# A decoder layer on one core: the attention steps written out, the gate work of a batch shifted to other slots

## The reference

```python
x = _layernorm(x + _L0_attn_ref(x, Wq, Wk, Wv))
x = _layernorm(x + _L0_xattn_ref(x, ctx, ctx, mask, W1, b1, W2, b2))
# in the experts: which two of eight, and with which weight
gate_scores = softmax(einsum('btd,ed->bte', x, Wg))
topk_val, topk_idx = top_k(gate_scores, 2)
topk_val = topk_val / (topk_val.sum(-1) + 1e-9)
comb = (one_hot(topk_idx, 8) * topk_val[..., None]).sum(-2)
x = _layernorm(x + sum_e comb[e] * ((a_e * sigmoid(b_e)) @ Wo.T + bo))
```

## Time and profile before

| | us |
|---|---|
| median of three runs | 1499.45 |
| the profiled execution | 1495.7 |
| its span, first to last instruction | 1493.9 |
| PE busy in the span | 1282.1 (86%) |
| DVE busy | 1142.6 (76%) |
| ACT busy | 756.8 (51%) |
| POOL busy | 656.1 (44%) |

### The profile page before, as it was taken

How to read it: one execution, slowest core, us unless ns; L and a number is a source line. 1 busy time by engine, 2 the same in 40 slices (tenths; PEclk the granted TensorE clock), 3 DMA queues, 4 the chain that set the end, 5 groups by cost and what they waited for, 6 DMA issues and landing times. The chain is left out here.

```text
span 1493.9 us, 32343 instructions
## 1 busy us (share of the span) xinstructions
PE 1282.1 (86%) x7668; PEld 903.5 (60%) x7669; DVE 1142.6 (76%) x3110; ACT 756.8 (51%) x1743; POOL 656.1 (44%) x1018
## 2 busy tenths in 40 slices
PE   6888999989899898989988505999999999968886
PEld 4443555555555555555543304888888888858786
DVE  1455788888788787878874467888888888859998
ACT  1125677777677677777777241323223232314444
POOL 1011244444454444444544472334343343447886
PEclk9998999999999999999998557999999999989999
DMA  4435456647556566566535721433434334369995
GB/s 100 105 60 100 80 107 131 122 103 131 114 113 126 113 119 116 119 124 112 118 87 181 273 94 58 133 135 130 137 128 136 131 129 138 129 239 318 338 331 200
DMA packets 171805, 211.34 MB, mean 141 GB/s; under 512 B 20048, under 2 KB 143056, under 8 KB 167632
## 3 DMA queue, kind: packets, MB, share of 16 engines
q1 hardware_dynamic: 147808, 143.92, 41.7%
q0 software_dynamic: 17680, 55.28, 9.9%
q10 hardware_dynamic: 6240, 11.34, 2.2%
HBM read 124.81 MB, written 84.89 MB: 140 GB/s over the span
## 5 line engine op out<-in xcount | busy, mean ns | idle before, releaser
L859 DVE TENSOR_REDUCE negmax<-psS 128x2 f32<-128x512 f32 x512 | 349.6, 687 | 109.0 <-PE psS L631 102.0
L761 ACT ACTIVATE probs<-psT 128x512 f32<-128x512 f32 x512 | 302.7, 597 | 190.3 <-PE psT L641 189.4
L631 PE MATMUL psS<-kstack,qstack 96*128 96x256 bf16 x1024 | 197.4, 275 | 50.7 <-DVE negmax L859 21.6
L1337 ACT ACTIVATE sig<-hb 128x512 f32<-128x512 f32 x136 | 86.0, 633 | 287.2 <-DVE hb L1420 281.6
L641 PE MATMUL psT<-qstack,kstack 99*128 99x512 bf16 x512 | 197.2, 386 | 5.1 <-ACT probs L761 5.1
L1217 POOL DMA_INDIRECT g_rows<-g,slot x136 | 135.5, 996 | 70.2 <-issue 66.9
L631 PEld LDWEIGHTS psS<-kstack,qstack 96*128 96x128 bf16 x1024 | 92.0, 104 | 109.9 <-DVE negmax L859 74.0
L397 POOL DMA_INDIRECT lists<-x,slots x128 | 127.0, 992 | 34.2 <-issue 30.3
L529 PE MATMUL psO<-probs,vaug 128*32 128x512 f32 x1024 | 140.0, 619 | 0.9 <-ACT probs L761 0.8
L1431 DVE SCALAR_TENSOR_TENSOR g<-g,xe,sig 128x512 f32<-128x512 f32 x136 | 102.3, 752 | 27.4 <-DVE g L1427 14.4
L1420 DVE TENSOR_TENSOR hb<-psHb,f_b 128x512 f32<-128x512 f32 x136 | 94.1, 692 | 36.6 <-issue 31.8
(11 more groups left out here) (201 smaller groups left out, 2962.8 us busy)
## 6 DMA issues: line engine op xcount, KB each, us to landing
rows<-g_rows SPq DMA_DIRECT2D x32, 1024.0 KB, 8.1
qstack<-q_parts SPq DMA_DIRECT2D x192, 128.0 KB
xe<-lists SPq DMA_DIRECT2D x136, 133.0 KB, 2.1
q_parts<-qpart SPq DMA_DIRECT2D x32, 384.0 KB, 2.8
sums<-x SPq DMA_DIRECT2D x32, 264.0 KB, 2.3
x2in<-sums SPq DMA_DIRECT2D x32, 264.0 KB, 5.0
xt<-in_x_t SPq DMA_DIRECT2D x32, 256.0 KB, 6.0
xres<-in_x SPq DMA_DIRECT2D x32, 256.0 KB, 3.2
```

Of the source, the lines that this page charges most:

```text
L631: last = mm(psS[:, u % 2, hh * S:(hh + 1) * S], qstack[0:KROWS, b1.s4, 2 * hp + hh, c * P:(c + 1) * P], kstack[0:KROWS, b1.s4, :], start=T ...
L761: nc.scalar.activation(probs[:, u % PT, :], psT[:, u % 2, :], ACT.Exp, scale=SELF_SCALE).then_inc(sm["exp_done"], 1)
L859: v.tensor_reduce(negmax[:, b1.s2, 2 * hp:2 * hp + 2, c], psS[:, u % 2, :].rearrange("p (h k) -> p h k", h=2), AX.X, ALU.max, negate=True) ...
```

## The change

The change has five parts.

- All 39 steps of the first phase are written out; the loop and its registers go. Which waits a PSUM bank's user makes is kept as it was (only the one for its predecessor in steps 8 to 31).
- The second norm's transposes move from slot 5 to 6 (behind the `probs` product with `vaug`), their copy from 6 to 7, the gate product from 7 to 8, the logits copy from 7 to 8, the best two from 8 to 9 and 9 to 10, ids from 10 to 11, the sum of the choices from 11 to 12, the ACT exponentials from 11 to 12, and the rest of the chain from 12, 13 and 14 to 13, 14 and 15.
- The gate weights and ids move from the end of step t to slot 6 of step t+1, and `chosen`, `slotf` and `slots` from slots 0 to 2 to slots 6 to 8, ahead of the logits copy.
- The four pieces that split the maxima move from slots 1 to 4 to slots 0 to 3.
- SP stores the rows of batch t-7 at the end of its step, behind the loads of `qstack`, and POOL waits for `slots` only behind both of its `qpart` operations.

```diff
 def pipeline(eng, step):
-    for r in range(8):
-        step(Step(0, r))
-    with eng.Fori(2, B // 4) as j:
-        for r in range(4):
-            step(Step(j, r))
-    for r in range(7):
-        step(Step(B // 4, r))
+    for n in range(B + 7):
+        step(Step(0, n))
 # SP
-            b = t.back(7)    # ahead of the xres load: wait comb_ready, store x2 rows
...
+            b = t.back(7)    # now behind the qstack loads
 # POOL
-                wait(pool, "slots_ready", done(b7))
                 wait(pool, "q_split", 2 * t.n + 1)
                 pool.tensor_tensor(qpart[:, t.s2, 2], qrest[:, t.s2], qpart[:, t.s2, 1], ALU.subtract
...
-                if not active(t):
-                    wait(pool, "slots_ready", done(b7))
+                wait(pool, "slots_ready", done(b7))
                 dispatch(b7, 0)
 # PE
-            for k in range(len(order)) if t.fixed else ((i - 1) % len(order),):
+            for k in range(len(order)) if not 8 <= t.n < B else ((i - 1) % len(order),):
-                if u == 5 and active(b6):    # x2 transposes
+                if u == 6 and active(b6):
-                if u == 7 and active(b6):    # gate product
+                if u == 8 and active(b6):
 # ACT
-                if u == 6 and active(b6):    # x2t copy
+                if u == 7 and active(b6):
-                if u == 11 and active(b6):   # gexp, gtop
+                if u == 12 and active(b6):
 # DVE
-                if 1 <= u <= 4 and active(b2):
-                    split_max(b2, u - 1)
+                if u <= 3 and active(b2):
+                    split_max(b2, u)
+                if u == 6 and active(b7):    # gate weights, ids; then chosen
+                if u == 7 and active(b7):    # slotf
+                if u == 8 and active(b7):    # slots, ahead of the logits
-                if u == 7 and active(b6):    # logits
+                if u == 8 and active(b6):
```

More of the change, by code:

```diff
@@ L315, in step @@
                 load_setup()
-            b = t.back(7)
[L317 to L321, removed]
             b = t.back(3)
@@ L348, in step @@
                                  ).then_inc(sm[f"q_stacked{b.s2}"], 16)
+            b = t.back(7)
+            if active(b):
+                wait(sp, "comb_ready", done(b))
+                rows = dram["sum"].rearrange("(b s) d -> b s d", s=S)[bass.ds(b.n, 1)]
+                sp.dma_start(rows.rearrange("o (c p) d -> p (o c) d", p=P), x2[:, b.s2, :, 0:D + E]
+                             ).then_inc(sm[f"x2_stored{b.s2}"], 16)
             if t.fixed:
@@ L851, in step @@
                     wait(dve, "stats2_ready", done(b6))
-                if u == 9 and active(b6):
+                if u == 10 and active(b6):
                     wait(dve, "gate_max", done(b6))
@@ L896, in step @@
                                     ).then_inc(sm["cross_masked"], 1)
-                if u == 7 and active(b6):
+                if u == 6 and active(b7):
+                    wait(dve, "gate_link", done(b7, 7, 7))
+                    wait(dve, "hot_ready", done(b7))
+                    for c in range(QC):
+                        v.scalar_tensor_tensor(x2[:, b7.s2, c, D:D + E], gexp[:, b7.s2, c, :],
+                                               gden[:, b7.s2, c:c + 1], hotsum[:, b7.s2, c, :], ALU.mult, ALU.mult)
+                    last = v.tensor_copy(x2[:, b7.s2, :, D + E + 1], topf[:, b7.s2, :, 0])
+                    if b7.n >= 2:
+                        last = v.tensor_scalar(x2[:, b7.s2, :, D + E], x2[:, b7.s2, :, D + E], float(4 * S), None,
+                                               ALU.add)
+                    last.then_inc(sm["comb_ready"], 1)
+                if u == 6 and active(b7):
+                    wait(dve, "slot_link", 3 * b7.n + 1)
+                    v.tensor_tensor(chosen[:, b7.s2], hot[:, b7.s2],
+                                    place[:, b7.s2].unsqueeze(2).to_broadcast([P, QC, 2, E]), ALU.mult
+                                    ).then_inc(sm["slot_link"], 1)
+                if u == 7 and active(b7):
+                    wait(dve, "slot_link", 3 * b7.n + 2)
+                    v.tensor_reduce(slotf[:, b7.s2], chosen[:, b7.s2], AX.X, ALU.add).then_inc(sm["slot_link"], 1)
+                if u == 8 and active(b7):
+                    wait(dve, "slot_link", 3 * b7.n + 3)
+                    v.tensor_copy(slots[:, b7.s2], slotf[:, b7.s2].rearrange("p c k -> p (c k)")
+                                  ).then_inc(sm["slots_ready"], 1)
+                if u == 8 and active(b6):
                     wait(dve, "gate_scored", done(b6))
@@ L903, in step @@
                     att_reciprocal(b4, 0)
-                if u == 8 and active(b6):
+                if u == 9 and active(b6):
                     gate(1)
@@ L917, in step @@
                     att_reciprocal(b4, 1)
-                if u == 10 and active(b6):
+                if u == 10 and active(b4):
+                    att_norm(b4, 1)
+                if u == 11 and active(b6):
                     gate(2)
                     v.tensor_copy(topf[:, b6.s2], topi[:, b6.s2, :, 0:2]).then_inc(sm["gate_link"], 1)
-                if u == 10 and active(b4):
-                    att_norm(b4, 1)
-                if u == 10 and active(b6):
+                if u == 11 and active(b6):
                     gate(3)
@@ L928, in step @@
                                     ).then_inc(sm["gate_link"], 1)
-                if u == 11 and active(b6):
+                if u == 12 and active(b6):
                     gate(4)
@@ L941, in step @@
                     stats(y1, stats1, b4, "stats1_ready")
-                if u == 12 and active(b6):
+                if u == 13 and active(b6):
                     wait(dve, "gate_exp", done(b6))
@@ L948, in step @@
                     moments(stats1, mv1, b4, "var1_ready")
-                if u == 13 and active(b6):
+                if u == 14 and active(b6):
                     gate(5)
@@ L959, in step @@
                     v.reciprocal(crec[:, b5.s2], csum[:, b5.s2]).then_inc(sm["crec_ready"], 1)
-                if u == 14 and active(b6):
-                    gate(6)
-                    v.reciprocal(gden[:, b6.s2], gden[:, b6.s2]).then_inc(sm["gate_link"], 1)
                 if u == 14 and active(b5):
@@ L969, in step @@
                     last.then_inc(sm["y2_ready"], 1)
+                if u == 15 and active(b6):
+                    gate(6)
+                    v.reciprocal(gden[:, b6.s2], gden[:, b6.s2]).then_inc(sm["gate_link"], 1)
             if t.fixed and t.n == 0:
@@ L974, in step @@
             if active(b6):
[L976 to L983, removed]
                 wait(dve, "counted", done(b6))
```

12 lines of the change are left out of this document (removed).

## The result

The changed kernel takes 1549.51 us (median of four runs, 1548.36 to 1550.89); before, it was 1498.69 us in the runs beside it (1492.17 to 1501.52). The ratio is 1.0343, 95% interval 1.0302 to 1.0384: slower. The profiled span went from 1493.9 to 1547.5 us, +53.6. The prediction was 1532.2 with a range of 1508 to 1550; the direction and the step were right, and 18 us of the change were missing (50.8 against 32.8), which puts the time at the range's upper edge.

A forecast was written before the change was run, and what follows sets the result against it. A ring through PE, ACT and DVE's key part was taken to bound each step; 26 x (0.79 + 0.94 + 0.03) = +45.8, -14.0 and +1 gave +32.8, so 1532.2 us, range 1508 to 1550.

The forecast's parts named there:

- The ring: Dependency cycle through PE, ACT's exponential and cast, and DVE's key part; additions lengthen each step: 0.79 + 0.94 + 0.03 us.
- Gate chain: Slots 5 to 9: PE's 1.11 us wait goes, new waits of 0.96 and 0.94 come; net +0.79 us a step.
- Exponentials: Gate exponentials on ACT, now between slot 11's exponential and the k and v casts: +0.94 us a step.
- DVE's pieces: Moved gate weights, ids, `chosen`, `slotf`, divisions and maxima pieces: free except one small piece ahead of the key part, +0.03 us.
- The loop: Steps 12 to 30: five loop returns with DVE stops cost 14.0 us; written out, -14.0 us.
- PE's two new pauses: PE waits 0.96 us for the x2t copy in slot 8 and 0.94 us for logits before the cross transposes.
- rival (c): PE's waits lower its clock in each step, 0.3 to 0.8 us over 26 steps: 1540 to 1552 us; chance 0.10.
- The sign that it named: A granted PE clock under 0.97 in the attention stretch would speak for the clock rival.
- the last steps: The last seven steps, without key chain: extra gate slots cost, shorter DVE list gives back; +1 us, bounds -3 and +5.
- (a): New waits are hidden and slot 5's gap goes, 1456.6 us; or moves are neutral, 1485.5 us; chance 0.08.
- (b): Half of it: only the ACT part on the ring, 1481 us (0.05), or only the gate part, 1507 us (0.06).
- (d): Written-out code stops as often as the loop did, so 14 us stay: 1546.2 us; chance 0.03.

The follow-up runs named there:

- e7_gexp_filled: The changed kernel with the gate exponentials back in slot 11 and the `psT` product of slots 7 and 8 done four times in gate steps: 1505.56 us.
- e8_both_back: The changed kernel with the gate chain back in slots 5, 6, 7 and 7 and the gate exponentials back in slot 11: 1481.11 us.
- e3_gate_back: The changed kernel with x2 transposes, `x2t` copy, gate product and logits copy back in slots 5, 6, 7 and 7: 1508.69 us.
- e1_flat: The kernel before the change with only its loop written out as 39 steps: 1470.71 us.

## Why the prediction was wrong, point by point

- The ring, 26 x 1.76: right in total (23.76 - 22.06 = 1.70), which is luck, for its terms were each off. Gate chain forecast 0.79; measured 1.03 (e7_gexp_filled against e8_both_back) and, with the exponentials moved, 0.87 (after against e3_gate_back) (0.12 too little stood in the forecast between the gate product and slot 8's `psS`: 1.36 us, 422.37 to 423.73, where I had 1.24). Exponentials forecast 0.94; 0.64 and 0.80. DVE's pieces forecast 0.03; 0.27. "One small piece more stands ahead of the key part" overlooked that `topf` and `hot`, a slot later, stand ahead of `krest`. Against this stood 0.24 a step that writing the steps out saves.
- The loop: -14.0 for the returns was right in the steps (13.8 in before's, none in e1_flat's). "Written-out code and loop body run equally fast" was a coincidence: the written-out steps that I compared make five extra waits for each use of a bank (0.17 us a step), and the loop body loses about as much (0.24) by something else, perhaps its registers. Written out with one wait, a step is 21.82.
- PE's two new pauses: 0.96 and 0.94 forecast, 0.97 and 0.97 found. `krest` waits 0.7 us a step, not 1, and PE's two stops at the step's turn are 1.32 together (0.50 and 0.82), not 1.7. POOL's longer wait for `slots` cost nothing, as forecast.
- The clock, the step that failed. The forecast put it at nothing, and rival (c), which had it, got 0.10 and a price of 0.3 to 0.8 us in each step. The runs show 1.5 to 3.1 us in ten steps of 26, 21.6 us in all. The measured 1549.5 lies in (c)'s 1540 to 1552, but by another path than (c) describes: most steps pay nothing, ten pay much. The sign that it named came: the granted clock over 440 to 480 us is 0.91. I had read the price from the 2 us behind a loop's return (0.61); a low stretch here is up to 6.7 us long. And "the trace at the present waits shows 1.00 throughout, so it has not begun yet" was taken as a reason against (c), when my own forecast put two pauses of 0.95 us within 3 us where there had been one. It also rests on one window of 40 us: in before's 26 steps the clock stood at 1.2 GHz for 10 us, each time behind one of the loop's returns. The Trainium skill (TensorE: Matmul & The Clock Gate, A second HAM failure mode) tells of another kernel in which PE's short idle times between groups of matmuls made the clock go back and forth between its two levels; the traces agree, with 51 us at the lower one.
- The account: 26 x 1.70 = 44.2, +21.6 for the clock, -13.8 for the returns: +52.0 of the 53.6 that the spans differ by. The rest: the steps ahead of the 26 ended 3.7 us earlier, and the last steps took 5.8 us longer, where the forecast had +1 and a bound of +5. That term was off too, and no run takes it apart.
- Rivals (a), (b) and (d) fell: both waits came, and no stop was left in the written-out code.

What stays open: why the low stretches come in two neighbouring steps of six in after, and in 19 of 26 when the step is 0.6 us shorter; and why the clock falls ahead of the second pause in some steps. No run here varies the step's length alone.

## What to carry to other kernels

When a change leaves a busy TensorE with a second pause of about 1 us within a few us of the first, add a term for the clock, sized by the length of a whole low stretch and not by a glimpse of one; here it was half as large as the ring's cost. In how many steps it falls due could not have been forecast from the trace of before. To separate the two, fill the pause with a product that is thrown away: if the time falls although PE does more, it was the clock. And price each moved operation by what it now stands directly ahead of, on the engine that closes the ring; small casts count there.

## What the runs showed of the hardware

- Taking work off the ring can gain nothing: with the exponentials back, the step was 0.64 us shorter and the time the same (1549.77 against 1549.51), since the time at 1.2 GHz doubled from 51 to 106 us. Filling the pauses gave back 44 us.
- A stretch of 6.7 us at 1.2 GHz cost 2.7 us, one of half that length 1.5: PE's products there last 0.63 instead of 0.38 us, but part of it falls into time in which PE would have waited.
- Waits that never block cost time: 0.17 us a step for the extra ones of PE.
- A loop that returns every fourth step cost 13.8 us in five returns; the same steps written out had none, and no stops of their own (e1_flat: 24 of the 26 steps within 0.01 us of 21.82).
